# Two maxima-row transfers merged into one, and the turn of the maxima two places later, in a one-core transformer block

## The chip, the cores and the metric

The program runs on 1 core of one Trainium2 chip. The metric is the device time of one execution in microseconds (us); smaller is better. The kernel before takes 1949.46 us, the median of 3 runs (1944.86 to 1951.01).

## The reference, cut to what matters

```python
def _attn(q, k, v):
    scale = 1.0 / math.sqrt(HEAD_DIM)
    scores = jnp.einsum('bqhd,bkhd->bhqk', q, k) * scale
    w = jax.nn.softmax(scores, axis=-1)
    out = jnp.einsum('bhqk,bkhd->bqhd', w, v)
...
# x: (16, 256, 512), 16 heads of 32, d_ff 2048, float32
xn = _adaln(x, noise_emb, ln1_w, ln1_b); q, k, v = split(xn @ qkv_w.T)
x = x + _attn(_rope(q), _rope(k), v) @ sa_out_w.T              # self attention
xn = _adaln(x, noise_emb, ln2_w, ln2_b)
x = x + _attn(_rope(xn @ q_w.T), _rope(context @ k_w.T), context @ v_w.T) @ ca_out_w.T
xn = _adaln(x, noise_emb, ln3_w, ln3_b)
x = x + gelu(xn @ ffn_w1.T + ffn_b1) @ ffn_w2.T + ffn_b2
```

## The kernel before

The kernel has two blocks. The first, some 1250 us, is attention: 16 batch items of self attention, then 16 of cross attention, 32 items in all, each with 16 heads. The second, some 690 us, is the feed-forward part and is not touched.

**Heads and groups.** In the attention block the heads of all items are one stream of 512, numbered n. Eight heads make a group, numbered G from 0 to 63 (two groups to an item), and four heads share one stack of queries and keys, `qT` and `kT`. Each head passes through TensorE twice. First `scores` (L603) multiplies queries and keys into a bank of `ps_s`; VectorE takes the negated maximum of each row (L850); ScalarE takes the exponential with its sum (L733, the step `total`). LAG = 13 heads later `weigh` (L622) multiplies the same stacks the other way round, into another bank, and ScalarE takes the final exponential into `prob` (L747). The final exponential needs no bias, because the shift (negated maximum minus the logarithm of the sum) is already in the product: it stands as two more rows of the query stack, rows 96 and 97 (`ROWS:MROWS`), opposite two rows of ones in the key stack. The value stands in two rows as a rounded part and its rest.

**How these rows come about, once a group.** ScalarE takes the logarithm of eight sums (`log`, L741). VectorE makes the shift and splits it into its two parts in `max_parts` (`max_split`, L858 to L863). TensorE turns that tile so that heads stand on partitions (`max_turn`, L610), ScalarE copies 16 rows of 256 values out of PSUM into `max_rows` (`max_copy`, L713), and ScalarE's queue issues the transfers into `qT` (`max_rows`, L723): before, one for each of the two parts, each 8 rows of 1 KB that become one row of the stack. The first `weigh` of the group waits for these transfers on the semaphore `max_rows_in`. Nothing else waits for them but the copy of the group after the next.

**What sets the order.** `stage_order` writes one list of steps by hand, and every engine walks that list and issues its own part of it in order. A place is a third of a head: at place 3n comes `scores` of head n, at 3n + 1 `weigh` of head n - 13, at 3n + 2 `total` of head n. Other steps are put at a place and follow what stands there. The chain of group G is at 24G + 24 (`log`), + 25 (split), + 30 (turn), + 31 (copy), + 32 (transfers); the group's first `weigh` is at 24G + 40. Between the heads stand the projections of later items (L589, L593), their rotation and its spill to memory, and the loads of the stacks (L990 to L998) from SyncE's queue.

**Banks.** `ps_s` has five banks, handed out in turn to `scores`, `weigh`, `max_turn` and `mix`; a user waits until the fifth before it has been read.

Of the kernel before, what the change touches and what calls it, by code (L numbers as in the profile page):

```python
# [8 lines left out]
F32 = mybir.dt.float32  # L9
# [25 lines left out]
def stage_order(B):  # L35
# [104 lines left out]
        if i == N - 2:  # L140
            weight_rows(p + 45, [("ffn", k, 0) for k in (0, 2, 4, 1, 3, 5, 6, 7)], 5, 15)
    for G in range(2 * N):
        for n, kind in ((24, "log"), (25, "max_split"), (30, "max_turn"), (31, "max_copy"), (32, "max_rows")):
            put(24 * G + n, kind, G)
    for quad in range(2, 4 * N):
        put(12 * quad - 20, "stack", "k", quad)
# [96 lines left out]
def block_kernel(nc, x, condT, ctxT, lnT, lnb, attnT, w1T, b1, w2T, b2, cos, sin, pick, ident_in, x1, x2, out):  # L243
# [5 lines left out]
    HG = H // 2  # L249
# [63 lines left out]
    with ExitStack() as whole:  # L313
# [37 lines left out]
        with ExitStack() as stage:  # L351
# [171 lines left out]
            def attention_tensor(eng):  # L523
                for step in order:
# [54 lines left out]
                    elif kind == "project":  # L579
                        m, i, t, c = step[1:]  # L580
                        layer = i // B
                        row = MATS.index(m) * KC + c
                        b = bank(("project", m, i, t, 0))
                        eng.wait_ge(*x_ready(m, i, c))
                        eng.wait_ge(w_split, nth["w_low", layer, m, c])
                        hi, lo = sides(m, i)
                        for j, (a, w) in enumerate(((hi, w_hi), (hi, w_lo), (lo, w_hi))):
                            if m in "vo":
                                ins = eng.matmul(ps_g[:, b, :], a[:, c, t * P:(t + 1) * P], w[:, row, :],  # L589
                                                 start=c == 0 and j == 0, stop=c == KC - 1 and j == 2)  # L590
                                continue
                            for s in range(2):
                                ins = eng.matmul(ps_g[:, b, s * L:(s + 1) * L], w[:, row, (T * s + t) * P:(T * s + t + 1) * P], a[:, c, :],  # L593
                                                 start=c == 0 and j == 0 and s == 0, stop=c == KC - 1 and j == 2, skip_group_check=True)
                        ins.then_inc(product_done if c == KC - 1 else rows_used, 1)
                    elif kind == "scores":
                        n = step[1]
                        quad, j = divmod(n, OH)
                        if j == 0:
                            for m in "kq":  # L600
                                eng.wait_ge(stack_in[m][quad % 4], 16 * STACKS[m] * (quad // 4 + 1))
                        for t in range(T):
                            ins = eng.matmul(ps_s[:, score_bank(step), t * L:(t + 1) * L], qT[0:ROWS, quad % NQ, j, t * P:(t + 1) * P],  # L603
                                             kT[0:ROWS, quad % NQ, j, :], start=True, stop=True)
                        ins.then_inc(scores_done, 1)
                    elif kind == "max_turn":
                        G = step[1]
                        eng.wait_ge(max_split, G + 1)
                        for t in range(T):
                            ins = eng.transpose(ps_s[0:2 * HG, score_bank(step), t * P:(t + 1) * P],  # L610
                                                max_parts[:, t, 0:2 * HG], ident[:, :])
                        ins.then_inc(max_turned, 1)
                    elif kind == "weigh":
                        n = step[1]
                        quad, j = divmod(n, OH)
                        if n % HG == 0:
                            G = n // HG
                            eng.wait_ge(max_rows_in[G % 2], 16 * 2 * (G // 2 + 1))
                        if n == 0:
                            eng.wait_ge(ones_set, 1)  # L620
                        for t in range(T):
                            ins = eng.matmul(ps_s[:, score_bank(step), t * L:(t + 1) * L], kT[:, quad % NQ, j, t * P:(t + 1) * P],  # L622
                                             qT[:, quad % NQ, j, :], start=True, stop=True)
                        ins.then_inc(weigh_done, 1)
                    elif kind == "mix":
                        G = step[1]
                        i, g = divmod(G, 2)
                        b = score_bank(step)
                        if g == 0:
                            eng.wait_ge(v_done, values[i, 1])  # L630
                        for c in (2 * g, 2 * g + 1):
                            eng.wait_ge(exp_done, OH * (KC * i + c + 1))
                            cols = slice((c % 2) * L, (c % 2 + 1) * L)
                            for k in range(T):
                                for j in range(OH):
                                    n = OH * (KC * i + c) + j
                                    ins = eng.matmul(ps_s[j * HD:(j + 1) * HD, b, cols],
                                                     v_sb[i % NV][:, k, c * P + j * HD:c * P + (j + 1) * HD],
                                                     prob[:, n % NP, k, :], start=k == 0, stop=k == T - 1)
                            ins.then_inc(mix_done, 1)  # L640

            def attention_scalar(eng):
# [3 lines left out]
                for step in order:  # L646
# [61 lines left out]
                    elif kind == "max_copy":  # L708
                        G = step[1]
                        eng.wait_ge(max_turned, G + 1)  # L710
                        if G >= 2:
                            eng.wait_ge(max_rows_in[G % 2], 16 * 2 * (G // 2))
                        eng.activation(max_rows[G % 2][:, :], ps_s[0:2 * HG, score_bank(("max_turn", G)), 0:L],  # L713
                                       ACT.Copy).then_inc(maxes_copied, 1)
                    elif kind == "max_rows":
                        G = step[1]
                        eng.wait_ge(maxes_copied, G + 1)
                        if G >= NQ // 2:
                            eng.wait_ge(weigh_done, HG * (G - NQ // 2 + 1))
                        first = 2 * G % NQ  # L720
                        for s in range(2):
                            into = qT[ROWS + s:ROWS + s + 1, first:first + 2, :, :]
                            eng.dma_start(into.rearrange("p g h l -> p (g h) l").bitcast(F32),  # L723
                                          max_rows[G % 2][s * HG:(s + 1) * HG, :].bitcast(F32)).then_inc(max_rows_in[G % 2], 16)
                    elif kind == "total":
                        n = step[1]
                        G, j = divmod(n, HG)
                        eng.wait_ge(max_done, n + 1)
                        if j == 0 and G >= 2:
                            eng.wait_ge(log_done, G - 1)  # L730
                        scores = ps_s[:, score_bank(("scores", n)), :]
                        for t in range(T):
                            ins = eng.activation(scores[:, t * L:(t + 1) * L], scores[:, t * L:(t + 1) * L], ACT.Exp,  # L733
                                                 bias=neg_max[G % 2][:, t, j:j + 1], accum_out=total[G % 2][:, t, j:j + 1])
                        ins.then_inc(total_done, 1)
                    elif kind == "log":
                        G = step[1]
                        eng.wait_ge(total_done, HG * (G + 1))
                        if G:
                            eng.wait_ge(shift_done, G)  # L740
                        eng.activation(log_sb[:, :, :], total[G % 2][:, :, :], ACT.Ln).then_inc(log_done, 1)  # L741
                    elif kind == "weigh":
                        n = step[1]
                        eng.wait_ge(weigh_done, n + 1)
                        if n >= NP:
                            eng.wait_ge(mix_done, (n - NP) // OH + 1)
                        eng.activation(prob[:, n % NP, :, :].rearrange("p t l -> p (t l)"), ps_s[:, score_bank(step), :],  # L747
                                       ACT.Exp).then_inc(exp_done, 1)
                    elif kind == "o_split":
                        G = step[1]  # L750
                        i, g = divmod(G, 2)
                        eng.wait_ge(mix_done, 2 * (G + 1))
                        if i and g == 0:
                            eng.wait_ge(product_done, products["o", i - 1, 1])
                        eng.activation(o_hi[:, 2 * g:2 * g + 2, :], ps_s[:, score_bank(("mix", G)), :].rearrange("p (c l) -> p c l", l=L),
                                       ACT.Copy).then_inc(o_hi_done, 1)
# [895 lines left out]
```

## Time and profile before

| | |
|---|---|
| median of 3 runs (lowest, highest) | 1949.46 us (1944.86, 1951.01) |
| the profiled execution's own time | 1946.9 us |
| span of its trace | 1945.1 us |
| granted TensorE clock, mean over the span | 0.989 |
| PE busy | 1878.5 us, 97% |
| ACT busy | 1388.9 us, 71% |
| DVE busy | 1298.7 us, 67% |
| POOL busy | 789.8 us, 41% |

In rows of the trace PE is TensorE's matmuls, PEld its weight loads, ACT ScalarE, DVE VectorE, POOL GpSimd. ACTq and SPq rows are transfers being issued by the sequencers of ScalarE and SyncE; their length is that of the issue, not of the data's way. What stands in brackets at a row's end is how long the engine was idle before it and what released it.

### The profile page before, as it was taken

What the parts mean: (1) busy time and instruction counts of PE and PEld (TensorE: products, weight loads), DVE (VectorE), ACT (ScalarE), POOL (GpSimd) and SP (SyncE); (2) the same over time, 40 slices, a digit from 0 to 9 for tenths busy, and PEclk for the clock granted to TensorE, in tenths of its full rate; (3) what the DMA queues carried; (4) which work ended last, traced back from release to release, by engine and by line L of the source; (5) the groups of instructions that cost most, each with busy time, mean ns of one, the idle gap of its engine ahead of it and who ended that gap; (6) DMA issues with size and microseconds to landing.
All of it is one profiled execution on the core that took longest, in us unless ns stands there. A gap on an engine that the chain in (4) does not pass through costs nothing. (4 is left out here: it accounts for less than half of the span.)

```text
span 1945.1 us, 39403 instructions
## 1 busy us (share of the span) xinstructions
PE 1878.5 (97%) x13460; PEld 1639.8 (84%) x13460; DVE 1298.7 (67%) x2248; ACT 1388.9 (71%) x3813; POOL 789.8 (41%) x820
## 2 busy tenths in 40 slices
PE   8799999999998999999999997899999999999999
PEld 6678888888887888888888875688898989999898
DVE  6766677676677677676776665446667676766754
ACT  3577778788877888888888886655656566565654
POOL 4433343343343454454454432013445354454531
PEclk9899999999999999999999998999999999999999
DMA  6766566666668667667667676253231323223130
GB/s 208 217 196 208 169 186 205 177 183 202 183 190 229 202 205 229 200 198 226 198 203 220 200 210 166 77 160 123 73 107 57 109 59 115 77 87 98 55 98 33
DMA packets 307348, 308.38 MB, mean 159 GB/s; under 512 B 21968, under 2 KB 260944, under 8 KB 307152
## 3 DMA queue, kind: packets, MB, share of 16 engines
q1 hardware_dynamic: 304528, 304.47, 51.8%
q8 instruction: 111, 1.82, 0.4%
q10 hardware_dynamic: 2624, 1.39, 0.3%
q14 instruction: 85, 0.70, 0.1%
HBM read 212.46 MB, written 92.27 MB: 157 GB/s over the span
## 5 line engine op out<-in xcount | busy, mean ns | idle before, releaser
L850 DVE TENSOR_REDUCE neg_max<-ps_s 128x2 f32<-128x512 f32 x512 | 350.2, 687 | 227.6 <-PE ps_s L603 227.3
L733 ACT ACTIVATE ps_s<-ps_s,neg_max 128x256 f32<-128x256 f32 x1024 | 455.1, 446 | 46.7 <-DVE neg_max L850 42.7
L747 ACT ACTIVATE prob<-ps_s 128x512 f32<-128x512 f32 x512 | 305.6, 597 | 136.8 <-PE ps_s L622 124.9
L914 POOL TENSOR_TENSOR rope_c<-rope_c,rope_s 128x256 f32<-128x256 f32 x128 | 98.0, 765 | 343.6 <-DVE rope_s L825 343.6
L622 PE MATMUL ps_s<-qT,kT 98*128 98x256 f32 x1024 | 215.5, 292 | 13.1 <-DMA qT<-max_rows 8.1
L603 PE MATMUL ps_s<-kT,qT 96*128 96x256 f32 x1024 | 213.6, 290 | 10.4 <-ACT ps_s L733 8.5
L603 PEld LDWEIGHTS ps_s<-kT,qT 96*128 96x128 f32 x1024 | 171.7, 191 | 55.8 <-ACT ps_s L733 22.7
L593 PE MATMUL ps_g<-xx_hi,w_hi 128*128 128x256 f32 x1024 | 209.8, 286 | 6.5 <-DVE rope_s L825 5.1
L733 ACT ACTIVATION_READ_ACCUMULATOR ps_s<-ps_s,neg_max 128x1 f32 x1024 | 209.9, 205 | 0.0
L593 PE MATMUL ps_g<-xx_lo,w_hi 128*128 128x256 f32 x1024 | 206.8, 284 | 0.0
L593 PE MATMUL ps_g<-xx_hi,w_lo 128*128 128x256 f32 x1024 | 206.7, 283 | 0.0
L1280 PE MATMUL ps_y<-w_hi,h_hi 128*128 128x512 f32 x512 | 201.5, 393 | 1.2 <-DVE h_lo L1405 1.2
L1280 PE MATMUL ps_y<-w_lo,h_hi 128*128 128x512 f32 x512 | 200.7, 392 | 0.0
L622 PEld LDWEIGHTS ps_s<-qT,kT 98*128 98x128 f32 x1024 | 170.0, 191 | 34.9 <-ACT ps_s L733 11.5
L1280 PE MATMUL ps_y<-w_hi,h_lo 128*128 128x512 f32 x512 | 199.3, 389 | 0.0
L1405 DVE TENSOR_TENSOR h_lo<-h_sb,h_hi 128x512 fp32r<-128x512 f32 x128 | 111.9, 878 | 104.4 <-ACT h_hi L1303 103.0
L921 POOL TENSOR_TENSOR rot_lo<-rope_c,rot_hi 128x512 fp32r<-128x512 f32 x128 | 167.1, 1306 | 28.9 <-ACT rot_hi L707 28.6
L902 POOL TENSOR_TENSOR xx_lo<-xT,xx_hi 128x512 fp32r<-128x512 f32 x68 | 89.6, 1319 | 217.3 <-ACT xx_hi L693 217.3
L593 PEld LDWEIGHTS ps_g<-xx_hi,w_hi 128*128 128x128 f32 x1024 | 159.8, 191 | 12.4 <-DVE rope_s L825 6.3
L1264 PE MATMUL ps_h<-xf_hi,cw_hi 128*128 128x256 f32 x592 | 167.5, 283 | 0.0
L1264 PE MATMUL ps_h<-xf_lo,cw_hi 128*128 128x256 f32 x592 | 165.8, 280 | 0.0
L1264 PE MATMUL ps_h<-xf_hi,cw_lo 128*128 128x256 f32 x592 | 165.7, 280 | 0.0
(154 smaller groups left out, 4666.6 us busy)
## 6 DMA issues: line engine op xcount, KB each, us to landing
kT<-k_turned SPq DMA_DIRECT2D x384, 128.0 KB, 3.0
qT<-q_turned SPq DMA_DIRECT2D x128, 256.0 KB, 3.7
f_raw<-in_w1T SPq DMA_DIRECT2D x124, 256.0 KB, 3.0
k_turned<-rot_hi SPq DMA_DIRECT2D x64, 256.0 KB, 3.2
k_turned<-rot_lo SPq DMA_DIRECT2D x64, 256.0 KB, 2.7
q_turned<-rot_hi SPq DMA_DIRECT2D x64, 256.0 KB, 3.4
q_turned<-rot_lo SPq DMA_DIRECT2D x64, 256.0 KB, 3.5
qT<-q_turned SPq DMA_DIRECT2D x128, 128.0 KB, 3.7
```

Of the source, the lines that this page charges most:

```text
L593: ins = eng.matmul(ps_g[:, b, s * L:(s + 1) * L], w[:, row, (T * s + t) * P:(T * s + t + 1) * P], a[:, c, :], start=c == 0 and j == 0 and ...
L603: ins = eng.matmul(ps_s[:, score_bank(step), t * L:(t + 1) * L], qT[0:ROWS, quad % NQ, j, t * P:(t + 1) * P], kT[0:ROWS, quad % NQ, j, :], ...
L622: ins = eng.matmul(ps_s[:, score_bank(step), t * L:(t + 1) * L], kT[:, quad % NQ, j, t * P:(t + 1) * P], qT[:, quad % NQ, j, :], start=Tru ...
L733: ins = eng.activation(scores[:, t * L:(t + 1) * L], scores[:, t * L:(t + 1) * L], ACT.Exp, bias=neg_max[G % 2][:, t, j:j + 1], accum_out= ...
L747: eng.activation(prob[:, n % NP, :, :].rearrange("p t l -> p (t l)"), ps_s[:, score_bank(step), :], ACT.Exp).then_inc(exp_done, 1)
L850: eng.tensor_reduce(neg_max[G % 2][:, :, j], ps_s[:, score_bank(step), :].rearrange("p (t l) -> p t l", l=L), AX.X, ALU.max, negate=True). ...
L902: eng.tensor_tensor(lo[:, ks, :], xT[:, ks, :], hi[:, ks, :].bitcast(F32), ALU.subtract).then_inc(x_low_done, 1)
L914: eng.tensor_tensor(rope_c[n % 2][:, 0, :], rope_c[n % 2][:, 0, :], rope_s[:, 0, :], ALU.subtract)
L921: eng.tensor_tensor(rot_lo[:, n % NT, :, :], rope_c[n % 2][:, :, :], rot_hi[:, n % NT, :, :].bitcast(F32), ALU.subtract).then_inc(rot_lo_d ...
L1264: ins = eng.matmul(ps_h[:, bank(p, n), 0:L], w[:, cols], x_[:, k, :], start=n in OPENS and k == 0 and j == 0, stop=k == 1 and j == 2, skip ...
L1280: ins = eng.matmul(ps_y[:, t, :], h[:, t * P:(t + 1) * P], w, start=c == 0 and j == 0, stop=c == FC - 1 and j == 2)
L1405: eng.tensor_tensor(h_lo[a % NH][:, :], h_sb[a % 2][:, :], h_hi[a % NH][:, :].bitcast(F32), ALU.subtract).then_inc(h_lo_done, 1)
```

## The change

The two transfers of a group become one, with 2 rows of the stack as its target and all 16 rows of `max_rows` as its source. So `max_rows_in` counts 16 a group where it counted 32. The turn, the copy and the transfer stand two places later in the list, at 24G + 32, + 33 and + 34. The logarithm and the split stay.

```diff
-        for n, kind in ((24, "log"), (25, "max_split"), (30, "max_turn"), (31, "max_copy"), (32, "max_rows")):
+        for n, kind in ((24, "log"), (25, "max_split"), (32, "max_turn"), (33, "max_copy"), (34, "max_rows")):
...
-                            eng.wait_ge(max_rows_in[G % 2], 16 * 2 * (G // 2 + 1))
+                            eng.wait_ge(max_rows_in[G % 2], 16 * (G // 2 + 1))
...
-                            eng.wait_ge(max_rows_in[G % 2], 16 * 2 * (G // 2))
+                            eng.wait_ge(max_rows_in[G % 2], 16 * (G // 2))
...
-                        for s in range(2):
-                            into = qT[ROWS + s:ROWS + s + 1, first:first + 2, :, :]
-                            eng.dma_start(into.rearrange("p g h l -> p (g h) l").bitcast(F32),
-                                          max_rows[G % 2][s * HG:(s + 1) * HG, :].bitcast(F32)).then_inc(max_rows_in[G % 2], 16)
+                        into = qT[ROWS:MROWS, first:first + 2, :, :]
+                        eng.dma_start(into.rearrange("p g h l -> p (g h) l").bitcast(F32),
+                                      max_rows[G % 2][:, :].bitcast(F32)).then_inc(max_rows_in[G % 2], 16)
```

In the changed kernel every line behind L720 has a number smaller by one: L722 is the transfer, L732 the exponential of `total`, L746 the one of `weigh`.

On ScalarE, around group 56, before. L733 here is `total` of head 458, L707 the rounding of a rotated query, the L747 behind the transfers the final exponential of head 446, and the group's first `weigh` is that of head 448, two exponentials on.

```order
L713 ACTIVATE max_rows<-ps_s 16x256 [waits max_rows_in0,max_turned]
L733 ACTIVATE ps_s,total<-ps_s,neg_max 128x256 [waits max_done]
L733 ACTIVATE ps_s,total<-ps_s,neg_max 128x256
L707 ACTIVATE rot_hi<-rope_c 128x512 [waits spilled_q1,rope_added]
L723 DMA qT<-max_rows 1x8x256 [waits weigh_done,maxes_copied]
L723 DMA qT<-max_rows 1x8x256
L747 ACTIVATE prob<-ps_s 128x512 [waits mix_done,weigh_done]
```

The same place now:

```order
L732 ACTIVATE ps_s,total<-ps_s,neg_max 128x256 [waits max_done]
L732 ACTIVATE ps_s,total<-ps_s,neg_max 128x256
L707 ACTIVATE rot_hi<-rope_c 128x512 [waits spilled_q1,rope_added]
L713 ACTIVATE max_rows<-ps_s 16x256 [waits max_rows_in0,max_turned]
L746 ACTIVATE prob<-ps_s 128x512 [waits mix_done,weigh_done]
L722 DMA qT<-max_rows 2x8x256 [waits weigh_done,maxes_copied]
```

The copy has moved behind the exponential of `total` and the rounding, and the transfer behind the final exponential of head 8G - 2, which itself waits for TensorE's `weigh` of that head.

On TensorE, around group 25 (L603 is `scores` of head 210, L622 `weigh` of head 197, L589 products of a projection), before:

```order
L603 MATMUL ps_s<-kT,qT 128x256 x2
L610 MATMUL ps_s<-ident,max_parts 16x128 x2
L622 MATMUL ps_s<-qT,kT 128x256 x2
L589 MATMUL ps_g<-w_hi,o_hi 128x512
L589 MATMUL ps_g<-w_lo,o_hi 128x512
L589 MATMUL ps_g<-w_hi,o_lo 128x512
L589 MATMUL ps_g<-w_hi,o_hi 128x512
L589 MATMUL ps_g<-w_lo,o_hi 128x512
L589 MATMUL ps_g<-w_hi,o_lo 128x512
L603 MATMUL ps_s<-kT,qT 128x256 x2
```

And now:

```order
L603 MATMUL ps_s<-kT,qT 128x256 x2
L622 MATMUL ps_s<-qT,kT 128x256 x2
L589 MATMUL ps_g<-w_hi,o_hi 128x512
L589 MATMUL ps_g<-w_lo,o_hi 128x512
L589 MATMUL ps_g<-w_hi,o_lo 128x512
L589 MATMUL ps_g<-w_hi,o_hi 128x512
L589 MATMUL ps_g<-w_lo,o_hi 128x512
L589 MATMUL ps_g<-w_hi,o_lo 128x512
L610 MATMUL ps_s<-ident,max_parts 16x128 x2
L603 MATMUL ps_s<-kT,qT 128x256 x2
```

The turn has moved behind a `weigh` and what of a projection stands with it, right ahead of the next `scores`.

## Rows read from the trace of the kernel before

**Rows 1.** The page: busy time, share of the span, instructions.
```profile
PE 1878.5 (97%) x13460; PEld 1639.8 (84%) x13460; DVE 1298.7 (67%) x2248; ACT 1388.9 (71%) x3813; POOL 789.8 (41%) x820
```
**Rows 2.** Windows: us, busy by engine (instructions), clock, DMA share, GB/s.
```profile
250.00:650.00 400.00, 386.27 (x3007) 334.97 (x3008) 283.90 (x509) 315.75 (x982) 157.77 (x163) 0.99 0.66 193
650.00:1200.00 550.00, 539.94 (x4269) 469.77 (x4267) 380.40 (x714) 464.17 (x1459) 247.17 (x252) 0.99 0.70 208
```
**Rows 3.** Waits of TensorE: total us, times, longest us.
```profile
PE ps_s L610 <- DVE max_parts L863: 14.5, 16, 7.0
...
PE ps_s L622 <- DMA qT<-max_rows: 8.1, 7, 2.2
```
**Rows 4.** Timeline, group 25: start us, us, engine line op [idle before <-releaser].
```profile
542.16 1.00 DVE L863 TENSOR_TENSOR max_parts<-shift,max_parts 128x16 f32<-128x16 f32 x1
...
543.31 0.38 PE L610 MATMUL ps_s<-ident,max_parts 128*16 128x128 f32 x2 [0.43 <-DVE max_parts L863]
...
547.50 0.60 ACT L747 ACTIVATE prob<-ps_s 128x512 f32<-128x512 f32 x1 [0.43 <-issue]
...
550.52 0.40 PE L622 MATMUL ps_s<-qT,kT 98*128 98x256 f32 x2
```
**Rows 5.** Timeline, group 58: second transfer's issue and first weighing.
```profile
1152.73 0.63 ACTq L723 DMA_DIRECT2D qT<-max_rows  x1
1153.47 0.60 ACT L747 ACTIVATE prob<-ps_s 128x512 f32<-128x512 f32 x1 [0.56 <-issue]
...
1155.03 0.50 PE L622 MATMUL ps_s<-qT,kT 98*128 98x256 f32 x2 [1.08 <-ACT ps_s L733]
```
**Rows 6.** Timeline, group 10: the same.
```profile
272.01 0.63 ACTq L723 DMA_DIRECT2D qT<-max_rows  x1
272.74 0.60 ACT L747 ACTIVATE prob<-ps_s 128x512 f32<-128x512 f32 x1 [0.55 <-PE ps_s L622]
...
275.87 0.48 PE L622 MATMUL ps_s<-qT,kT 98*128 98x256 f32 x2 [0.70 <-DMA qT<-max_rows]
```
**Rows 7.** Page part 3 (packets, MB, share of 16 engines), and issues.
```profile
q1 hardware_dynamic: 304528, 304.47, 51.8%
...
qT<-max_rows ACTq DMA_DIRECT2D x128, 8.0 KB
```
**Rows 8.** Timeline, group 56: transfers, the exponential behind them, spill, first weighing.
```profile
1118.41 0.66 ACTq L723 DMA_DIRECT2D qT<-max_rows  x1
...
1119.10 0.64 ACTq L723 DMA_DIRECT2D qT<-max_rows  x1
...
1119.84 0.60 ACT L747 ACTIVATE prob<-ps_s 128x512 f32<-128x512 f32 x1
...
1119.30 0.54 SPq L979 DMA_DIRECT2D k_turned<-rot_lo  x1
1119.94 0.82 SPq L990 DMA_DIRECT2D qT<-q_turned  x1
...
1122.09 0.40 PE L622 MATMUL ps_s<-qT,kT 98*128 98x256 f32 x2
```
**Rows 9.** Windows, group 56; the columns of Rows 2.
```profile
1118.00:1118.50 0.50, 0.50 (x6) 0.50 (x5) 0.02 (x1) 0.50 (x3) 0.50 (x2) 1.00 0.00 0
...
1121.00:1121.50 0.50, 0.50 (x7) 0.50 (x6) 0.50 (x2) 0.50 (x3) 0.50 (x1) 1.00 0.93 320
```
**Rows 10.** Timeline, group 55: the same pair of rows.
```profile
1099.66 0.68 ACTq L723 DMA_DIRECT2D qT<-max_rows  x1
...
1101.50 0.58 ACT L747 ACTIVATE prob<-ps_s 128x512 f32<-128x512 f32 x1
...
1104.42 0.40 PE L622 MATMUL ps_s<-qT,kT 98*128 98x256 f32 x2
```
**Rows 11.** Timeline, group 61's turn; matmuls of group 58 at either clock.
```profile
1205.96 0.58 PE L610 MATMUL ps_s<-ident,max_parts 128*16 128x128 f32 x2 [6.96 <-DVE max_parts L863]
...
1149.35 0.63 PE L593 MATMUL ps_g<-xx_hi,w_lo 128*128 128x256 f32 x2
...
1151.20 0.40 PE L593 MATMUL ps_g<-xx_hi,w_lo 128*128 128x256 f32 x2
```

## The prediction

> **What bounds the kernel now.** I read the page's busy times first, then the windows of the attention block, then TensorE's waits, then single groups in the timeline. TensorE is busy 97% of the span [rows 1]; in the two long stretches of attention it is busy 386 of 400 and 540 of 550 us, at a granted clock of 0.99, while ScalarE has 316 and 464 us and VectorE less [rows 2]. So TensorE is the bound, and the edit is worth what it adds to or takes from TensorE's idle time, nothing more. Of that idle time two kinds belong to the chain that is edited [rows 3]: the turn waits for VectorE's split, 14.5 us in 16 waits, and the first weighing of a group waits for the transfers, 8.1 us in 7 waits. More waits of the second kind are put down to another releaser, as in group 58, where 1.08 us is charged to an exponential that had long been done [rows 5]. Counting each place where the first weighing starts late, I find 12 groups of 64, from 0.3 to 2.3 us. Matmuls that follow one another overlap by 0.16 us in the rows, so a wait shown as 0.43 us moves the end by about 0.6.
>
> **The turn.** In the 12 odd groups 3 to 25 the turn stands at TensorE's head while the split is still running: 0.43 us idle in group 25 [rows 4], 0.43 to 0.46 in the others. Two places later it stands behind a weighing and six projection products, some 1.6 us of work, and the split, which ended 0.15 us ahead of the turn, is then long done. 12 x 0.61 = -7.3 us (between -7.3 and -4, if a later wait takes some back). Four more groups have turn waits of 0.4 to 1.3 us, and group 61 one of 6.96 us [rows 11]; there nothing but one weighing can slip ahead of it, so 0.3 to 0.5 us is saved. With those: -2.5 us (0 to -3.3).
>
> **The transfer: when it is issued.** Before, ScalarE's sequencer issued the pair as soon as the copy was done, ahead of the final exponential of head 8G - 2. Now it meets that exponential first, and must hold there until TensorE has done its weighing. In the traces a transfer is issued within 0.07 us of the start of what precedes it, so I set the new issue at the start of that exponential plus 0.07. In group 56 that is 1119.91, where the second old issue began at 1119.10: 0.8 us later, 1.5 later than the first [rows 8]. The first weighing is at 1122.09: a window of 2.18 us. In group 55 the window is 1104.42 - 1101.57 = 2.85 us [rows 10], in group 25 it is 550.52 - 547.57 = 2.95 [rows 4]. In group 10 it is 275.87 - 272.81 = 3.06 us with a stall of 0.70 + 0.16 in it, so 2.2 without [rows 6].
>
> **The transfer: how long it takes.** The shortest way from issue to first weighing with TensorE waiting is 1155.03 - 1152.73 = 2.30 us, in group 58 with the transfer engines quiet [rows 5]. In group 10, in a burst of other transfers, it is 275.87 - 272.01 = 3.86 us [rows 6]. One transfer of 16 KB is not quite one of 8 KB [rows 7]: each is 8 pieces of 1 KB, and all 16 now belong to one instruction whose target has an outer dimension of 2 where both sides had 8. No row shows how the pieces of such a shape are spread. A packet of the main queue takes 0.518 x 16 x 1945.1 us / 304528 = 0.053 us [rows 7]. All at once costs nothing more; all 16 in one line 15 x 0.053 = 0.8 us; I take the middle, two lines of eight, 7 x 0.053 = +0.37 us. So 2.67 us in quiet, and up to 3.9 in a burst.
>
> The Trainium skill, "DMA: Bandwidth & Descriptors", section "Why a DMA increments its semaphore by 16 and not by 1", says that a transfer is spread over the largest number of engines, at most 16, that divides the slowest dimension of both sides. By that rule the two old transfers ran on 8 engines each and the new one runs on 2, eight pieces in a row, which would give the middle value above. No row here shows a transfer of such a shape, so the rule speaks against this change without being borne out yet.
>
> **By kinds of groups.** (A) The 13 groups 30, 32 and 36 to 56, even: window 2.18 us, no wait at present. The old pair went out while the engines were idle (share 0.00 at 1118.0); the new one's data moves 1.3 us after its issue, at 1121.2, where the share is 0.93, because the spill and the load of a stack were issued at 1119.30 and 1119.94 [rows 8, 9]. It is the start of a burst, not its height, so I take 3.0 us, between 2.67 and 3.86: a stall of 0.82, 13 x 0.82 = +10.7 us (at 2.3: +1.6; at 3.6: +18.5). (B) The 9 even groups 8 to 24: window 2.2; the burst that delays group 10 now is partly over 0.8 us later. Four at 2.7 (stall 0.5) and five at 3.1 (0.9) are 6.5 us, against 2.9 us of stalls now: +3.6 us (-1.5 to +9). (C) The 14 odd groups 31 to 57: window 2.85, data in the tail of a burst, 3.1 us: stalls of some 0.2, +2.8 us (0 to +7). (D) The odd early groups, window 2.95 against 2.67: nothing (0 to +3). (E) Eight groups where ScalarE itself runs late (1, 26, 27, 28, 34, 58, 60, 62), so that the exponential starts 1.5 to 2.5 us ahead of the weighing: in group 58 the window is 1155.03 - 1153.54 = 1.49 [rows 5], so 2.67 gives +1.2. For all eight I put +7 us (3 to 10).
>
> **ScalarE.** One issue of 0.63 us a group falls away; it shows as idle time of 0.4 to 0.6 us [rows 4, 5] in about half of the groups. TensorE's work covers that except where ScalarE is behind, five or six groups: -1 us (0 to -3). Were ScalarE the bound, it would be some 15. The copy of 0.36 us only changes place, and its later bank release is met by no user before the next `scores` but two.
>
> **The sum.** -7.3 - 2.5 + 10.7 + 3.6 + 2.8 + 7.0 - 1.0 = +13.3 us. On the profiled execution, 1946.9 us with a span of 1945.1, that is 1960.2; it lay 2.6 us under the median of the runs, which I take as the base: 1949.5 + 13.3, about 1963 us. What is late next is plain: the stall of the turn is moved to the first weighing, two heads on, with interest.
>
> **The rivals.** (1) The transfer comes in time: its pieces go out side by side and meet no queue in (A). Then A is 1.6, B 0, C 0, E 3.5, with -7.3 - 2.5 - 1: -5.7 us, 1944 us. For it: group 58's 2.30 us. Against it: the share of 0.93 just when the data would move. It decides at 2.2 us from issue to weighing in the even groups. (2) Savings and stalls cancel, with about 2.7 us in (A): A 6.8, B 1, C 1, E 4, less 10.8: +2, some 1951.5 us. (3) The transfer waits through the whole burst: A 18.5, B 9, C 7, E 10, less 10.8: +33.7, 1983 us. For it: 3.86 in group 10; against it: a spill issued only 0.6 us ahead. (4) The clock: after the 0.9 us idle ahead of group 58 the same pair of products takes 0.63 us instead of 0.40, the level of 1.2 GHz instead of 2.4 [rows 11]. Stalls of A's size do that nowhere alone (group 10 keeps its clock), but in E they fall together; three more falls of 6.8 us at half rate are +10 on top of my sum: 1973 us. (5) The edit does not do what it says, if the transfer was never held by the exponential because that was issued long before; then only the turn's part is left, which is close to (1).
>
> **How the numbers follow.** Forecast 0.40; (1) with (5) 0.15; (2) 0.22; (3) 0.13; (4) 0.10. Less than 0.3%, 5.8 us, can't be told from no change. 1944 lies at that edge, so (1) gives 0.12 to faster and 0.03 to the middle; (2) gives 0.19 to the middle and 0.03 to slower; with the others slower is 0.66. The range runs from 1948 to 1980 us: (1) and most of (3) are left out.
>
> **What would show it.** Right: the turn's wait for L863 falls from 14.5 us to 7 or 8, with no idle time ahead of L610 in groups 3 to 25. The first weighing's idle time rises from 8.1 us by the transfer (16 by my count) to 30 to 40, with a wait in every even group, 0.6 to 0.9 us each from group 30 on. Wrong: no wait in the even groups from 30 on, so the transfer takes under 2.2 us; or waits over 1.3 us there, so it queues behind the whole burst; or the exponential (L746) starting earlier than before, against the weighing. In a quiet stretch, group 62 for one, the way from issue to weighing tells whether the merged transfer itself is longer than 2.3 us.

## The result, and the profile after

| | before | after |
|---|---|---|
| median of 5 runs (lowest, highest) | 1949.46 us (1944.86, 1953.14) | 1960.07 us (1958.39, 1965.69) |
| the profiled execution's own time | 1946.9 us | 1958.39 us |
| span of its trace | 1945.1 us | 1956.6 us |
| granted TensorE clock, mean | 0.989 | 0.989 |

The changed kernel is slower: ratio 1.0069 with a 95% interval of 1.0051 to 1.0086. The medians lie 10.6 us apart, the profiled executions 11.5 us. The forecast was 1963 us, in a range of 1948 to 1980.

The page of the changed kernel, its busy times [against rows 1], and its window over the longer of the two stretches of attention [against rows 2]:

```profile
PE 1883.3 (96%) x13460; PEld 1636.8 (84%) x13460; DVE 1296.4 (66%) x2248; ACT 1390.0 (71%) x3813; POOL 789.6 (40%) x820
```

```profile
650.00:1200.00 550.00, 534.66 (x4202) 462.61 (x4200) 375.08 (x706) 456.10 (x1432) 243.17 (x249) 1.00 0.68 203
```

The work is the same, and what is lost is lost mainly behind 650 us: there 4202 matmuls fit into 550 us where 4269 did. The first weighings say the same. The one of group 25 starts 4.8 us earlier than before (545.74 against 550.52 [rows 4]), the one of group 56 10.0 us later (1132.07 against 1122.09 [rows 8]). The clock is not the reason, it is 1.00 there. (The feed-forward part is as long as before, 695 us.)

The waits of TensorE in the changed kernel (total us, times, longest us):

```profile
PE ps_s L622 <- DMA qT<-max_rows: 18.6, 20, 4.1
PE ps_s L603 <- ACT ps_s L732: 13.0, 19, 2.2
PE ps_s L622 <- ACT ps_s L732: 6.7, 10, 2.4
PE ps_s L610 <- DVE max_parts L862: 4.3, 2, 3.8
```

Before, the first and the last of these were 8.1 us in 7 waits and 14.5 us in 16 [rows 3]. The view puts the second and third down to the exponential of `total`, which frees a bank. For first weighings that is not always so: in the trace's record of the semaphores the transfer's own count comes last at all 27 late first weighings of the changed kernel. Before, the second and third were:

```profile
PE ps_s L603 <- ACT ps_s L733: 8.5, 8, 2.3
PE ps_s L622 <- ACT ps_s L733: 4.3, 8, 1.1
```

**The turn, group 25** [against rows 4]. Timeline of the changed kernel, TensorE's and ScalarE's rows:

```profile
539.75 0.38 PE L610 MATMUL ps_s<-ident,max_parts 128*16 128x128 f32 x2
...
540.27 0.50 PE L603 MATMUL ps_s<-kT,qT 96*128 96x256 f32 x2
...
542.75 0.65 ACTq L722 DMA_DIRECT2D qT<-max_rows  x1
...
545.74 0.40 PE L622 MATMUL ps_s<-qT,kT 98*128 98x256 f32 x2
```

The wait of 0.43 us ahead of the turn is gone. But the next `scores` starts 0.52 us after the turn, and the turn takes 0.38: a gap of 0.14 us stands there now, 0.30 with the overlap. The transfer has 2.99 us to the first weighing and holds nobody.

**The transfer, groups 56 and 36.** The spill is the 256 KB transfer from `rot_lo` to memory. Group 56 [against rows 8] first, then group 36, to which the experiments return:

```profile
1128.83 0.54 SPq L978 DMA_DIRECT2D k_turned<-rot_lo  x1
1129.01 0.57 ACT L746 ACTIVATE prob<-ps_s 128x512 f32<-128x512 f32 x1
1129.14 0.62 ACTq L722 DMA_DIRECT2D qT<-max_rows  x1
1129.47 1.52 SPq L989 DMA_DIRECT2D qT<-q_turned  x1
...
1132.07 0.47 PE L622 MATMUL ps_s<-qT,kT 98*128 98x256 f32 x2 [0.31 <-DMA qT<-max_rows]
```

```profile
765.25 0.36 ACT L713 ACTIVATE max_rows<-ps_s 16x256 fp32r<-16x256 f32 x1
765.33 0.54 SPq L978 DMA_DIRECT2D k_turned<-rot_lo  x1
...
765.64 0.65 ACTq L722 DMA_DIRECT2D qT<-max_rows  x1
...
768.66 0.47 PE L622 MATMUL ps_s<-qT,kT 98*128 98x256 f32 x2 [0.40 <-DMA qT<-max_rows]
```

Before, both transfers of group 56 were issued ahead of the spill from `rot_lo` at 1119.30, and there was no wait [rows 8]. Now the one transfer is issued 0.31 us behind that spill, and from issue to first weighing it takes 2.93 us in group 56 and 3.02 us in group 36. The windows around the issue of group 36 in the changed kernel show what it meets [against rows 9]:

```profile
766.00:766.50 0.50, 0.50 (x7) 0.50 (x6) 0.50 (x2) 0.25 (x2) 0.00 (x0) 1.00 0.00 0
766.50:767.00 0.50, 0.50 (x6) 0.50 (x6) 0.50 (x2) 0.50 (x3) 0.16 (x1) 1.00 0.87 303
```

The share is 0.00 up to 0.9 us after the issue at 765.64, and 0.87 from there: that is the spill's data. The transfer's data comes into the middle of it. By the trace's record of single packets its first piece starts 1.64 us after the issue, where it is 1.27 us in group 58 with the engines quiet, and its last write ends at 2.33 us, where it is 1.71.

**In quiet, group 58** [against rows 5]:

```profile
1162.60 0.62 ACTq L722 DMA_DIRECT2D qT<-max_rows  x1
...
1165.00 0.47 PE L622 MATMUL ps_s<-qT,kT 98*128 98x256 f32 x2 [1.62 <-DMA qT<-max_rows]
```

In group 58, where TensorE waits and no burst stands in the way, the merged transfer takes 2.40 us. The 2.30 us of the kernel before [rows 5] is not to be set against it, because there the weighing at 1155.03 waited for a bank. The last `total` that frees it ended at 1154.98, and the pair's semaphore was complete 0.38 us ahead of the weighing:

```profile
1154.77 0.21 ACT L733 ACTIVATION_READ_ACCUMULATOR ps_s<-ps_s,neg_max 128x1 f32 x1
```

So that wait was rightly charged to L733. A wait that the second of two old transfers does end, with the engines quiet, is in group 62 of the kernel with two late transfers (the experiment "Places alone"):

```profile
1287.80 1.31 ACTq L723 DMA_DIRECT2D qT<-max_rows  x2
...
1290.54 0.47 PE L622 MATMUL ps_s<-qT,kT 98*128 98x256 f32 x2 [1.38 <-DMA qT<-max_rows]
```

The row of 1.31 us holds both issues, the second 0.69 us behind the first, at 1288.49: 2.05 us from issue to weighing. The merged transfer is 0.35 us longer.

**All waits, counted by place.** These are all starts of TensorE that came late, with 0.16 us of overlap added to each:

| where TensorE waits | before, us | after, us | change |
|---|---|---|---|
| first weighing of a group | 13.3 (14 groups) | 26.2 (27 groups) | +12.9 |
| turn | 19.1 | 4.7 | -14.4 |
| `scores`, for a bank of an earlier `total` | 12.4 | 19.3 | +6.9 |
| other weighings | 3.3 | 6.4 | +3.1 |
| all, with those not named here | 72.6 | 81.3 | +8.7 |

Of the 13.3 us before, 2.9 us (groups 27, 34, 58 and 62) ended with a bank and not with the transfer, by the semaphores. The span grew by 11.5 us, so 2.8 us are in no single wait. Time at 1.2 GHz is 44.4 us in both traces.

### The profile page after: what moved, and what is told of

Same layout as the page of the kernel before. It is cut to its first block and busy times, and to the rows that moved or that the text cites. A ratio compares the mean times of both kernels' runs of the same rounds, so it can differ in the third digit from the quotient of the medians.

```text
span 1956.6 us, 39339 instructions
## 1 busy us (share of the span) xinstructions
PE 1883.3 (96%) x13460; PEld 1636.8 (84%) x13460; DVE 1296.4 (66%) x2248; ACT 1390.0 (71%) x3813; POOL 789.6 (40%) x820
## 5 line engine op out<-in xcount | busy, mean ns | idle before, releaser
L732 ACT ACTIVATE ps_s<-ps_s,neg_max 128x256 f32<-128x256 f32 x1024 | 455.5, 446 | 63.2 <-DVE neg_max L849 48.4
L746 ACT ACTIVATE prob<-ps_s 128x512 f32<-128x512 f32 x512 | 303.8, 594 | 126.8 <-PE ps_s L622 124.3
L622 PE MATMUL ps_s<-qT,kT 98*128 98x256 f32 x1024 | 211.0, 288 | 26.5 <-DMA qT<-max_rows 18.6
L603 PE MATMUL ps_s<-kT,qT 96*128 96x256 f32 x1024 | 219.9, 297 | 15.1 <-ACT ps_s L732 13.0
L603 PEld LDWEIGHTS ps_s<-kT,qT 96*128 96x128 f32 x1024 | 169.7, 192 | 63.8 <-ACT ps_s L732 27.9
L622 PEld LDWEIGHTS ps_s<-qT,kT 98*128 98x128 f32 x1024 | 170.4, 191 | 50.2 <-ACT ps_s L732 18.5
L732 ACT ACTIVATION_READ_ACCUMULATOR ps_s<-ps_s,neg_max 128x1 f32 x1024 | 208.9, 204 | 0.0
```

## The experiments

All ratios are to the kernel before, on the same chip. "Places" are those of turn, copy and transfers in the list: 30, 31, 32 before and 32, 33, 34 in the change. Where a kernel has one merged transfer, lines behind L720 are smaller by one, as in the changed kernel. "Merged" stands for the edits to the transfer and its three counts:

```diff
-                        for s in range(2):
-                            into = qT[ROWS + s:ROWS + s + 1, first:first + 2, :, :]
...
+                        into = qT[ROWS:MROWS, first:first + 2, :, :]
```

The theory at the outset: the time is lost because the late transfer comes into the burst that the spill opens, so that it needs 3.0 us where 2.4 are there. Rivals: the merged shape itself is slow; or the late turn and copy cost something by themselves. Kinds A to E are the prediction's kinds of groups.

### Merged alone

The merged edit, places 30, 31, 32.

> One transfer instead of two, turn, copy and transfer at their old places (30, 31, 32). Against the kernel before. Theory A (the late issue costs the time; merging alone saves an issue of 0.68 us and costs 0.23 us in flight): stalls at the first weighings fall from 13.3 us to 8 to 11, no new ones in the even groups from 30 on, time 2 to 4 us below the kernel before (ratio 0.998 to 0.999). Theory B (the merged transfer's spread over few engines costs the time): waits of 0.3 to 0.6 us in the even groups from 30 on, time 5 to 10 us above.

Measured: 1944.34 us (1939.93 to 1948.12, 12 runs), before 1947.88; ratio 0.9978 [0.9966, 0.9991]. Group 36 in the timeline:

```profile
758.82 0.65 ACTq L722 DMA_DIRECT2D qT<-max_rows  x1
...
759.71 0.54 SPq L978 DMA_DIRECT2D k_turned<-rot_lo  x1
...
762.49 0.40 PE L622 MATMUL ps_s<-qT,kT 98*128 98x256 f32 x2
```

Merging by itself makes the kernel faster, so the shape alone is not to blame: issued 0.89 us ahead of the spill the transfer holds nobody in group 36, and the stalls at first weighings fall from 13.3 to 8.7 us. The last byte no longer hangs on a second issue 0.69 us later. By the semaphores the pair of group 36 was complete 2.63 us behind its first issue before, and the merged transfer is complete after 2.25. Of the 4.6 us, 1.6 are in the four groups that waited for a bank before, so that part is ScalarE being done sooner.

### Places alone

```diff
-        for n, kind in ((24, "log"), (25, "max_split"), (30, "max_turn"), (31, "max_copy"), (32, "max_rows")):
+        for n, kind in ((24, "log"), (25, "max_split"), (32, "max_turn"), (33, "max_copy"), (34, "max_rows")):
```

> Two transfers as before, turn, copy and transfers at the new places (32, 33, 34). Theory A: the second issue comes some 0.68 us behind the merged one would and lands after 2.3 instead of 2.53 us, so the first weighings start 0.4 to 0.5 us later than in the changed kernel in some 20 to 25 groups: stalls of 35 to 40 us, time 17 to 22 us above the kernel before. Theory B: no slower than the kernel before by more than 3 us. Theory C (the order of the turn on TensorE and of the banks costs the time, not the transfers): the same 8 to 12 us above as the changed kernel.

Measured: 1998.44 us (1991.04 to 2005.57, 5 runs); ratio 1.0267 [1.0246, 1.0288], +52 us: the right sign, far outside what I expected. Waits, and group 36:

```profile
PE ps_s L622 <- DMA qT<-max_rows: 51.8, 39, 5.0
```

```profile
796.42 0.54 SPq L979 DMA_DIRECT2D k_turned<-rot_lo  x1
...
796.73 1.31 ACTq L723 DMA_DIRECT2D qT<-max_rows  x2
797.06 0.87 SPq L990 DMA_DIRECT2D qT<-q_turned  x1
...
801.50 0.48 PE L622 MATMUL ps_s<-qT,kT 98*128 98x256 f32 x2 [2.15 <-DMA qT<-max_rows]
```

The row of 1.31 us holds both issues, so the second begins about 797.4, behind the spill and behind the load of a stack as well. It reaches the weighing 4.1 us later; the merged one, issued between the two, took 3.0. Group 36 is the worst of the 13 groups of kind A, whose median is 3.5 us. By my count first weighings wait some 60 us in 46 groups, 46 more than before. And such waits cost the clock. A window of this kernel, then of the kernel before over the same times (the clock stands third from the end, 0.83 against 0.93):

```profile
600.00:650.00 50.00, 38.18 (x255) 30.51 (x254) 30.32 (x52) 31.48 (x94) 12.32 (x12) 0.83 0.68 191
```

```profile
600.00:650.00 50.00, 44.29 (x326) 37.70 (x325) 36.17 (x65) 35.97 (x108) 21.31 (x21) 0.93 0.68 185
```

TensorE had 85.3 us at 1.2 GHz in this trace against 44.4; half of the 41 us more, some 20, is lost work. 46 + 20 less the 9 us that the turn brings on balance is about the 58.6 us by which this trace's span exceeds that of before. But this trace is of the longest of the five executions (2005.57 us, mean clock 0.979). The other four had 0.983 to 0.986, which is 56 to 68 us at 1.2 GHz, so in the median the clock's part is nearer 8 us. Both parts were missing from my expectation: the longer way of a second transfer, and the clock.

### Turn alone, two transfers

Places 32, 31, 32: the turn is late, copy and transfers stand where they stood and wait for it there.

```diff
-        for n, kind in ((24, "log"), (25, "max_split"), (30, "max_turn"), (31, "max_copy"), (32, "max_rows")):
+        for n, kind in ((24, "log"), (25, "max_split"), (32, "max_turn"), (31, "max_copy"), (32, "max_rows")):
```

> Two transfers as before; only TensorE's turn is two places later (turn 32, copy 31, transfers 32 on ScalarE as before). Theory A: the copy starts at the same time as before or 0.2 us later, because ScalarE came to it late anyway; the turn's stalls fall by 12 x 0.3 to 0.6 us, those of the first weighings stay near 13 us: 3 to 6 us below the kernel before. Theory C: the waits of the scores for their banks (7 us more in the changed kernel) and the loss of 10 us come with the turn alone: 5 to 10 us above.

Measured: 1948.40 us (1945.67 to 1953.82, 12 runs), before 1947.88; ratio 1.0011 [1.0000, 1.0022]. My expectation, a gain, was missed. Waits, and group 25:

```profile
PE ps_s L603 <- ACT ps_s L733: 11.7, 21, 2.3
PE ps_s L622 <- ACT ps_s L733: 7.9, 12, 1.3
```

```profile
542.18 0.38 PE L610 MATMUL ps_s<-ident,max_parts 128*16 128x128 f32 x2
...
542.75 0.51 PE L603 MATMUL ps_s<-kT,qT 96*128 96x256 f32 x2 [0.18 <-ACT ps_s L733]
```

By my count the turn's own waits fall from 19.1 to 5.5 us, but those of `scores` rise from 12.4 to 17.9, of other weighings from 3.3 to 5.8, and of first weighings from 13.3 to 14.3. In the odd early groups 0.61 us ahead of the turn becomes 0.34 us ahead of the next `scores`: with TensorE no longer held, it reaches a bank that `total` of an earlier head still reads. Of the turn's 13.6 us, 9.0 go back, over half, and 5.5 of them at `scores`.

### Merged, only the issue late

The merged edit, turn and copy as before, the transfer behind the final exponential.

```diff
-        for n, kind in ((24, "log"), (25, "max_split"), (30, "max_turn"), (31, "max_copy"), (32, "max_rows")):
+        for n, kind in ((24, "log"), (25, "max_split"), (30, "max_turn"), (31, "max_copy"), (34, "max_rows")):
```

> One transfer; turn and copy at the old places (30, 31), only the issue of the transfer at 34, behind the final exponential of head 8G - 2. Theory A: the transfer is issued as late as in the changed kernel or up to 0.3 us later, so the first weighings stall 26 to 34 us; the turn keeps its 19 us of stalls: 12 to 20 us above the kernel before, above the changed kernel too. Theory C: within 3 us of the kernel before. If instead the issue goes out before the exponential has started, stalls stay under 15 us and the late copy, not the exponential, is what holds the transfer in the changed kernel.

Measured: 1957.54 us (1955.93 to 1958.85, 6 runs); ratio 1.0054 [1.0042, 1.0066], +9.7 us, where I expected 12 at the least. First weighings wait 22.5 us by my count (26 to 34 expected), 9.0 of them in kind A. Group 36:

```profile
765.34 0.35 ACT L713 ACTIVATE max_rows<-ps_s 16x256 fp32r<-16x256 f32 x1
...
766.80 0.65 ACTq L722 DMA_DIRECT2D qT<-max_rows  x1
...
770.01 0.47 PE L622 MATMUL ps_s<-qT,kT 98*128 98x256 f32 x2 [0.45 <-DMA qT<-max_rows]
```

The copy is done at 765.69, and the issue still goes out only at 766.80, 0.22 us ahead of the exponential's own start (767.02): the hold that I predicted exists. Against merged alone the late issue costs 13.2 us, between medians of the same chip. So a late issue costs this much by itself, with turn and copy where they were.

### The changed kernel with the issue ahead of the exponential

The diff is against the changed kernel.

```diff
-        for n, kind in ((24, "log"), (25, "max_split"), (32, "max_turn"), (33, "max_copy"), (34, "max_rows")):
+        for n, kind in ((24, "log"), (25, "max_split"), (32, "max_turn"), (33, "max_copy"), (33, "max_rows")):
```

> The changed kernel with the transfer at place 33 instead of 34: issued right behind the copy, ahead of the final exponential of head 8G - 2. Theory A1 (in the changed kernel the transfer is held by the late copy, which ends as that exponential starts): nothing changes from group 30 on, only the even groups up to 28 gain 0 to 0.4 us; 8 to 11 us above the kernel before, as the changed kernel is (10.6). Theory A2 (it is held by the exponential): stalls of the even groups from 30 on fall from 0.5 us to under 0.2, time at most 5 us above the kernel before.

Measured: 1960.32 us (1952.27 to 1960.76, 5 runs), before 1947.75; ratio 1.0060 [1.0046, 1.0074]. It is like the changed kernel. (Its trace is of the shortest of the five executions, 1952.27 us, and has 24.2 us at first weighings.) Group 36:

```profile
763.20 0.36 ACT L713 ACTIVATE max_rows<-ps_s 16x256 fp32r<-16x256 f32 x1
763.28 0.54 SPq L978 DMA_DIRECT2D k_turned<-rot_lo  x1
763.58 0.65 ACTq L722 DMA_DIRECT2D qT<-max_rows  x1
...
766.56 0.47 PE L622 MATMUL ps_s<-qT,kT 98*128 98x256 f32 x2 [0.35 <-DMA qT<-max_rows]
```

The issue follows the copy's end by 0.02 us, with no exponential between, and yet it is behind the spill and 2.98 us ahead of the weighing, as in the change (3.02). Once the copy is at place 33, the copy holds the transfer, and the exponential, which runs beside it, hardly adds to that.

### Merged, turn late, copy and transfer early

Merged, places 32, 31, 32, so the diff of the experiment with the turn alone and the merged edit.

> One transfer; only the turn is two places later (turn 32, copy 31, transfer 32). If the effects of the two parts add up, merging (-4 us) and turning later alone (+1 us, -2.4 up to group 25 and +2 behind it), it is 2 to 5 us below the kernel before. If the later turn costs by making the copy later, it is within 2 us of the kernel before.

Measured: 1941.42 us (1938.58 to 1943.42, 5 runs), before 1947.75; ratio 0.9967 [0.9955, 0.9980]. Waits:

```profile
PE ps_s L603 <- ACT ps_s L732: 13.3, 23, 2.5
...
PE ps_s L622 <- DMA qT<-max_rows: 3.4, 3, 1.8
```

First weighings wait 8.4 us, the turn 4.3. The kernel is 6 us faster than before, a little more than I expected. Only copy and transfer stand two places earlier here than in the change, and that is worth 1.0069 - 0.9967, about 1.0%, or 20 us: the late copy and transfer undo more than merging brings. The late turn brings at most 0.1% on top of merging, and as the intervals of 0.9967 and 0.9978 overlap, it isn't shown to bring anything. The table sets the two edits against each other:

| places (turn, copy, transfer) | two transfers | merged |
|---|---|---|
| 30, 31, 32 | 1 | 0.9978 |
| 32, 31, 32 | 1.0011 | 0.9967 |
| 32, 33, 34 | 1.0267 | 1.0069 |

With copy and transfer late merging is worth far more, 2.0% against 0.2% and 0.4%, two values that can't be told apart.

### The turn late only where the split holds it

Merged; the turn goes to 32 in odd groups 3 to 25 alone. It puts one more line ahead, so all lines are one higher than in the other merged kernels.

```diff
+        turn = 32 if G % 2 and 3 <= G <= 25 else 30
+        for n, kind in ((24, "log"), (25, "max_split"), (turn, "max_turn"), (31, "max_copy"), (32, "max_rows")):
```

> One transfer, copy and transfer at the old places; the turn two places later in the odd groups 3 to 25 alone, where it stood waiting for the split. Theory: there 0.61 us of stall at the turn become the 0.34 us that the next scores wait for their bank, 12 x 0.27 = 3.2 us less than with the merged transfer alone; nothing is lost in the late groups: 5 to 9 us below the kernel before (ratio 0.995 to 0.997). If the stall only moves on, it is as the merged transfer alone, 3 to 4 us below.

Measured: 1940.29 us (1938.58 to 1944.66, 5 runs), before 1947.75; ratio 0.9967 [0.9954, 0.9980]. Waits:

```profile
PE ps_s L604 <- ACT ps_s L733: 11.2, 22, 2.3
PE ps_s L611 <- DVE max_parts L863: 10.0, 5, 7.6
```

It beats the kernel before by 0.33%, some 6.5 us, and the changed one by 1%, and can't be told from the one of the experiment ahead. The other groups' turns gain little by going late: against that experiment the turn waits 8.5 us more, and `scores` and weighings 5.6 us less. Against merging alone the turn waits 7.9 us less and `scores` 4.5 more, the 3 us that I expected, but the intervals of 0.9967 and 0.9978 overlap.

### The changed kernel with a small spill, and its control

The spill from `rot_lo` moves 16 of 128 partitions from the third item on; seven eighths of the rotated rests are left out, so the memory holds old ones there. The control is the kernel before with the same cut.

```diff
-                        eng.dma_start(out_to[1], rot_lo[:, n % NT, :, :].bitcast(F32)).then_inc(spilled[m][t], 16)
+                        few = 16 if i >= 2 else P
+                        eng.dma_start(out_to[1][0:few], rot_lo[0:few, n % NT, :, :].bitcast(F32)).then_inc(spilled[m][t], 16)
```

> The changed kernel, but from item 2 on the spill of the rotated rests (the transfer from rot_lo) carries 16 of its 128 partitions; the other seven eighths are left out of the computation. In the changed kernel this spill is what runs when the merged transfer's data would move, in the even groups from 30 on. Theory A (queueing behind the spill delays the transfer): there the way from issue to first weighing falls from 3.0 us to 2.4 to 2.6, the stall of 0.5 us to 0 to 0.15 us, stalls at the first weighings in all from 26 us to 10 to 18, time 6 to 14 us below the changed kernel, so 0 to 5 us above the kernel before. Theory D (the way is as long by itself in these groups, 3.0 us, whatever else moves): stalls stay at 0.4 to 0.5 us in each, time within 4 us of the changed kernel.

> The same cut of the spill in the kernel before (seven eighths of the rotated rests left out from item 2 on): the control for the changed kernel with the cut. Before, no even group from 30 on waits for its transfer, so Theory A expects little: 1 to 6 us below the kernel before, from the groups where TensorE or ScalarE wait for transfers anyway (26 to 28, 60). Against this control the changed kernel with the cut should be 0 to 6 us slower under Theory A, 8 to 13 us under Theory D.

Measured: the changed kernel with the cut 1948.21 us (1943.45 to 1951.62, 10 runs), before 1947.40; ratio 1.0004 [0.9991, 1.0017]. The control 1947.75 us (1944.36 to 1949.41, 10 runs); ratio 0.9996 [0.9986, 1.0006]. Group 36 of the first:

```profile
761.22 0.65 ACTq L722 DMA_DIRECT2D qT<-max_rows  x1
...
763.69 0.40 PE L622 MATMUL ps_s<-qT,kT 98*128 98x256 f32 x2
```

The cut alone brings nothing, but with it nearly all of the change's loss is gone. The transfer is as late as before, and its 2.47 us suffice now: of the 13 groups of kind A all but two are without a wait, and those two have 0.12 and 0.13 us. The waits at first weighings are 15.8 us, against 26.2 with the whole spill; 7.2 us of that difference are in kind A. The mechanism is thereby shown for kind A: a late transfer costs because it shares the engines with the spill.

What this doesn't separate is the spill from the merged shape. The kernel with two late transfers issues the first of its pair at the same spot, 0.31 us behind the spill. By its semaphore that transfer of 8 KB is complete 2.31 us after its issue in the middle of the 13 groups, where the merged one is complete after 2.85 (2.25 with the engines quiet). A weighing starts 0.14 us behind a completion, and the issue stands 2.46 us ahead of the unhindered weighing. So an estimate from these rows is that a transfer spread as widely as the old ones would have come just in time there. It carried half of the bytes, and no run tries all 16 KB spread that way.

## Why the prediction was right, and where it wasn't

**The mechanism holds, and the number is partly luck.** TensorE is the bound; the turn's stall shrinks and another opens at the first weighing, above all in the even groups from 30 on. The sum said +13.3 us, and it is +11.5 between the profiled executions. But two misses of some size cancel. The first weighings were to wait 24.1 us longer and wait 12.9 longer; turn and ScalarE were to bring 10.8 us, and the turn brings 4.4 on balance. (The prediction counted 16 us at first weighings before; by the count of the table it is 13.3.)

**The turn, predicted -9.8 us.** At the turn itself it is -14.4 us, more than forecast, chiefly by group 61, whose wait fell from 6.96 us to 3.77 where I allowed 0.5. But the `scores` behind it wait 6.9 us more and the other weighings 3.1: net -4.4. The step that failed is "12 x 0.61", for which I named a later wait that takes some back, down to -4, and then counted it at nothing. Of 0.61 us 0.34 comes back, ahead of the next `scores`. By the ratios the late turn is worth 0.1% on top of merging, some 2 us, which is not clear of the noise.

**The exponential as what holds the issue.** This step was half wrong. It does hold it when the copy is early (the issue-late kernel), but the copy is late as well, and in the change either alone is enough (issue ahead: no gain). Also I took the start of that exponential from the trace of before, where it stood behind the two issues, 1119.84 in group 56. Without them it starts at 1129.01, 0.26 us behind the copy's start, and the transfer goes out at 1129.14. That is 2.46 us ahead of the unhindered weighing (1132.07 less a wait of 0.47), where I had 2.18 [rows 8].

**Kind A, +10.7 us.** The way of 3.0 us was right (2.93 and 3.02 in the rows above, 2.75 to 3.28 in 12 of the 13 groups; the choice "the start of a burst, not its height"). Its parts were not: it is 2.40 in quiet and 0.6 by the burst, and I had 2.67 and 0.33. The window was 2.46 us, and so 13 groups wait 7.5 us together, not 10.7. The error in the window is 0.28 x 13 = 3.6 us; one wait of 1.50 us, in group 54, gives some of it back.

**Kinds B, C, D.** B was put at +3.6 and is -0.7 (2.2 us after, 2.9 before). Here too the window was too short in my sum, 2.2 us where it is 2.59, as group 10 shows (2.89 us from issue to weighing, 0.30 of them wait), and the way in quiet is shorter than my 2.7. C, +2.8, is +0.7: the window is 3.13 us in most of these groups and not 2.85, and two of them wait, 0.60 and 0.11 us. D is 0, as said.

**Kind E, +7.0 us.** It is +5.4 (15.8 after, 10.4 before). In group 58 the way was 2.40 us instead of 2.67. The window up to the unhindered weighing was 0.62 us. My 1.49 had the old wait of 1.24 in it and leaves 0.25. ScalarE sends the transfer sooner than I had it, probably because it is freed of the second issue.

**The length of the merged transfer.** I took two lines of eight pieces and +0.37 us, and that is right: it is +0.35 from issue to weighing (2.05 to 2.40), and +0.25 to the end of the last write (1.46 to 1.71). What was wrong is the 2.30 us to which I added it, by the reading that group 58's exponential "had long been done". It had ended 0.05 us ahead of the weighing. So 2.67 us in quiet should have been 2.4. The transfer queue of ScalarE, in part 3 of the page, before and then after (packets, MB, share of 16 engines):

```profile
q10 hardware_dynamic: 2624, 1.39, 0.3%
```

```profile
q10 hardware_dynamic: 1728, 1.39, 0.3%
```

The same bytes in 896 packets fewer, 14 for each of 64 groups. The Trainium skill, "DMA: Bandwidth & Descriptors", section "Why a DMA increments its semaphore by 16 and not by 1", would have each old transfer on 8 engines and the new one on 2, and says that each engine that takes part ends with a write of its own to the semaphore: 16 writes a pair before, 2 now. The count agrees with it: 16 - 2 = 14. The semaphore's record agrees as well, with 8 separate writes for each old transfer and 2 for the new one. So the rule held. Its price was 0.35 us in quiet, and by the estimate under the small spill it may be what makes the transfer late in kind A.

**ScalarE, -1 us.** Undersized, because a path is missing. Merging alone is worth 3.5 us, and first weighings wait 4.6 us less. Of these, 1.6 are in groups that waited for ScalarE's bank, which is the path that I had; the rest is there because the second issue stood between the copy and the last byte. I costed the removed issue as work and not as delay of the data.

**The rivals.** (1), in time, is what happens with a small spill and hardly anywhere else. (2), some 2.7 us in kind A, is met by two of the 13 groups (2.75). (3), waits over 1.3 us, is met by group 54 (1.50) and by the second of two late transfers. (4), the clock, did not come in the change, where single waits of kind A are under 1 us with one exception (1.50); it came in the kernel with two late transfers, in its traced execution above all. (5) is out: with the transfer early the kernel is 20 us faster. What stays open is the 2.8 us of the span in no single wait. TensorE's busy time is 4.8 us larger, and its rows behind a wait are longer (0.47 where 0.40 is usual), which may be the same thing.

## What to carry to other kernels

Price a moved transfer by what is issued just ahead of it on the other queues: 0.3 us behind a spill cost the merged transfer 0.6 us of way, and a second transfer behind a load as well cost 1.4 in the median and 2.0 in group 36, while the issue itself was only about a microsecond later. Count a removed stall as won only when the next resource on that engine is free, here a bank. Merging two small transfers on which somebody waits saves the second's issue, here 0.69 us, less what a narrower spread costs, here 0.35; take that and leave the moves alone where they bring the transfer into a burst. And before a wait is taken for the time of a transfer, look whether it ended with the transfer or with a bank.

## What the runs showed that I had not expected

- Two small transfers in place of one, issued 0.65 us apart beside a burst, cost 2.0% of the time: the second takes 3.5 us from its issue in the median of kind A (4.1 in group 36) where the merged one takes 3.0.
- In the traced execution with two late transfers, 41 us more at 1.2 GHz came with waits of 1.3 us in the mean (51.8 us in 39), spread over many groups; in its four others it was 12 to 24 us more. Behind such a wait this is what a row looks like in the kernel with two late transfers, the projection product at half the clock:

```profile
761.92 0.48 PE L622 MATMUL ps_s<-qT,kT 98*128 98x256 f32 x2 [1.82 <-DMA qT<-max_rows]
...
762.63 0.63 PE L593 MATMUL ps_g<-xx_hi,w_lo 128*128 128x256 f32 x2
```

- A transfer whose 16 pieces run on 2 engines ended its last write only 0.25 us later than one of 8 pieces on 8, with the engines quiet. Beside the spill its semaphore was complete 0.54 us later (2.85 against 2.31).
- The shortest way read from the trace of before, 2.30 us, was the time of a bank and not of a transfer.
